# Routing tokens to experts in two parts, beside the experts' own work

## What is computed

```python
xm = layernorm(x) * gamma + beta                 # 6250 x 256
logits = xm @ Wr + br               # 8 experts, the best two of them per token
gate = softmax over the two chosen logits
y_k = gelu(xm @ W1[e_k] + b1[e_k]) @ W2[e_k] + b2[e_k]     # k = 1, 2; 256 -> 512 -> 256
out = x + gate_1 * y_1 + gate_2 * y_2
```

## Time and profile before

| what | value |
|---|---|
| median of 3 runs | 6035.27 us (6032.69 to 6035.34) |
| the profiled execution | 6032.18 us |
| its span, first to last instruction | 6030.5 us |
| granted TensorE clock, mean of the span | 0.766 of full speed |
| busy in the span | PE 55%, PEld 40%, DVE 46%, ACT 35%, POOL 62% |

### The profile page before, as it was taken

How to read it: one execution, slowest core, us unless ns; L and a number is a source line. 1 busy time by engine, 2 the same in 40 slices (tenths; PEclk the granted TensorE clock), 3 DMA queues, 4 the chain that set the end, 5 groups by cost and what they waited for, 6 DMA issues and landing times. The chain is left out here.

```text
span 6030.5 us, 75495 instructions
## 1 busy us (share of the span) xinstructions
PE 3346.5 (55%) x13479; PEld 2417.9 (40%) x13480; DVE 2750.8 (46%) x6682; ACT 2082.8 (35%) x5020; POOL 3748.8 (62%) x3707
## 2 busy tenths in 40 slices
PE   4355555555646666665834753056666664229990
PEld 1144444344434444443723752034444443216660
DVE  6655555532234444443544353555555557402223
ACT  4433333332333333332311310055555554313331
POOL 4266666666766666665777777777777773530006
PEclk7577777777967777777977987578888885569995
DMA  2233333333133333334211211011111115241114
GB/s 73 91 96 93 94 94 94 92 96 70 39 84 101 99 100 100 101 99 84 36 18 10 46 31 14 4 27 27 27 27 27 27 27 116 83 161 55 56 55 131
DMA packets 280618, 407.59 MB, mean 68 GB/s; under 512 B 93991, under 2 KB 197765, under 8 KB 280262
## 3 DMA queue, kind: packets, MB, share of 16 engines
q0 software_dynamic: 142720, 275.10, 19.7%
q1 hardware_dynamic: 137798, 131.50, 7.1%
HBM read 323.82 MB, written 81.61 MB: 67 GB/s over the span
## 5 line engine op out<-in xcount | busy, mean ns | idle before, releaser
L1156 PE MATMUL conv_ps<-conv_msg,conv_S 128*128 128x256 f32 x3328 | 1202.6, 536 | 991.6 <-DMA conv_msg<-relu_xn_table,GI 521.4
L1156 PEld LDWEIGHTS conv_ps<-conv_msg,conv_S 128*128 128x128 f32 x3328 | 907.0, 281 | 1314.5 <-issue 1121.2
L1128 DVE TENSOR_TENSOR ACC<-ACC,conv_ps 128x256 f32 x1664 | 700.9, 421 | 1190.0 <-PE conv_ps L1156 1082.6
L683 POOL DMA_INDIRECT edges_by_src<-packed,rank_i x800 | 953.9, 1192 | 308.9 <-issue 240.9
L1079 POOL DMA_INDIRECT conv_msg<-relu_xn_table,GI x832 | 800.4, 962 | 430.3 <-issue 235.3
L1079 POOL DMA_INDIRECT conv_msg<-conv_table,GI x832 | 788.2, 947 | 380.0 <-issue 233.9
L1852 POOL DMA_INDIRECT gat_msg<-attn_table,GI x832 | 824.9, 992 | 266.6 <-issue 253.3
L1099 ACT ACTIVATE conv_S<-iota_row,LOC 128x128 f32<-128x128 f32 x1664 | 507.9, 388 | 890.9 <-PE conv_ps L1156 806.2
L1905 PE MATMUL gat_ps<-gat_M,gat_S 128*128 128x260 f32 x1664 | 600.1, 509 | 373.9 <-DVE ACC L1959 223.4
L1905 PEld LDWEIGHTS gat_ps<-gat_M,gat_S 128*128 128x128 f32 x1664 | 378.6, 247 | 519.5 <-issue 463.1
L2508 POOL DMA_INDIRECT combine_y<-expert_out,combine_at x98 | 94.2, 961 | 578.5 <-ACTq L2496 557.2
(11 more groups left out here) (428 smaller groups left out, 5116.8 us busy)
## 6 DMA issues: line engine op xcount, KB each, us to landing
expert_in<-heads_zrow SPq DMA_DIRECT2D x53, 256.0 KB
experts_xe<-expert_in SPq DMA_DIRECT2D x106, 128.0 KB
expert_out<-experts_y SPq DMA_DIRECT2D x106, 128.0 KB, 1.7
conv_msg<-relu_xn_table,GI POOLq DMA_INDIRECT x832, 2.7
conv_msg<-conv_table,GI POOLq DMA_INDIRECT x832, 2.7
gat_msg<-attn_table,GI POOLq DMA_INDIRECT x832
edges_by_src<-packed,rank_i POOLq DMA_INDIRECT x800, 3.1
relu_xn_table<-begin_rx SPq DMA_DIRECT2D x49, 128.0 KB, 1.7
```

Source lines behind the costliest of these rows:

```text
L683: pool.indirect_dma_start(edges, bass.IndirectOffsetOnAxis(ap=m.rank_i[:, j:j + 1], axis=0), m.packed[:, j:j + 1], None).then_inc(sent[g % ...
L1128: nc.vector.tensor_tensor(acc, acc, ps[k % NB][:, 0:D], ALU.add).then_inc(added, 1)
L1156: nc.tensor.matmul(ps[k % NB][:, 0:D], S[:, h % 2, k, :], msg[:, h * RING + k, :], start=True, stop=True).then_inc(summed, 1)
```

## The change

The 49 row tiles are split into a first part of 25 and a second of 24 (`PART`). Each part has its own DRAM tables and its own padding: `EX_PART` is [58, 56], so there are 114 expert tiles instead of 106. The scan, the padding and the expert numbers are computed for each part in turn. The dispatch stage sends only the first part; its weights are issued from ScalarE's queue, beside it. In the experts stage, while the tiles of part one are worked, SyncE loads the second part's row tiles (one after every second expert tile) and GpSimd sends them. Once all 58 result tiles of part one are stored, GpSimd gathers the results of the first 24 row tiles (`BESIDE`), VectorE forms their sums between the tiles of part two (`collect`, after every second tile), and SyncE stores them. The combine stage does the remaining 25. The copies of positions into `at` are gone: the indirect DMAs read `pos_i` itself. SyncE's and GpSimd's lists are written out without loops.

```diff
-EX_TILES = ((2 * N + EXPERTS * (P - 1)) // P + 1) // 2 * 2
+PART = 25
+PART_ROWS = (PART * P, N - PART * P)
+EX_PART = [((2 * rows + EXPERTS * (P - 1)) // P + 1) // 2 * 2 for rows in PART_ROWS]
+EX_TILES = sum(EX_PART)
+BESIDE = 24
 RING = 8
...
-            rows = m.expert_in.rearrange("(t p a) d -> t p (a d)", p=P, a=2)
-            for k in range(EX_TILES // 2):
-                sp.dma_start(rows[k], zrow[:, :]).then_inc(zero_out, 16)
+            for h in range(2):
+                rows = m.expert_in[h].rearrange("(t p a) d -> t p (a d)", p=P, a=2)
+                for k in range(EX_PART[h] // 2):
+                    sp.dma_start(rows[k], zrow[:, :]).then_inc(zero_out, 16)
...
+            for h, (lo, hi) in enumerate(((0, PART), (PART, TILES))):
+                a, b, w, n = scan, other, 1, hi - lo
+                while w < n:
+                    v.drain()
...
+                nc.vector.tensor_scalar(cnt[:, :], a[:, hi - 1, :], float(P - 1), None, ALU.add)
+                nc.vector.tensor_tensor(pre[:, lo:hi, :], pre[:, lo:hi, :], a[:, lo:hi, :], ALU.add)
...
+                ex_lo, ex_n = sum(EX_PART[:h]), EX_PART[h]
+                nc.vector.tensor_tensor(sp8[:, :], x[:, :], nt[:, :], ALU.subtract)
+                nc.vector.tensor_tensor(cmp[:, 0:ex_n, :], x[0:1, :].unsqueeze(1).broadcast_to([1, ex_n, EXPERTS]),
+                                        m.iota_row[0:1, 0:ex_n].unsqueeze(2).broadcast_to([1, ex_n, EXPERTS]), ALU.is_le)
...
+                nc.vector.tensor_tensor(pre[:, lo:hi, :], pre[:, lo:hi, :],
+                                        sp8[:, :].unsqueeze(1).broadcast_to([P, n, EXPERTS]), ALU.add)
...
+def send_rows(nc, m, pool, i, xm, sent):
+
+    for k in range(2):
+        pool.indirect_dma_start(m.expert_in[part_of(i)], bass.IndirectOffsetOnAxis(ap=m.pos_i[0:rows_of(i), k, i:i + 1], axis=0),
+                                xm[0:rows_of(i), :], None).then_inc(sent, 16)
+
+
+def fetch_rows(nc, m, pool, i, pair, got):
+
+    for k, y in enumerate(pair):
+        pool.indirect_dma_start(y[0:rows_of(i), :], None, m.expert_out[part_of(i)],
+                                bass.IndirectOffsetOnAxis(ap=m.pos_i[0:rows_of(i), k, i:i + 1], axis=0)).then_inc(got, 16)
+
...
         def _(sp):
-            def load(i, s, rows):
-                if reused_of_four(i):
-                    sp.wait_ge(sent[s], 2 * dma_count_of_four(i - 4, s))
-                    held(sp, ts)
-                sp.dma_start(xm[s][:, :], m.xm[bass.ds(i * P, P), :]).then_inc(xm_in[s], 16)
-
-            over_tiles_by_four(sp, load)
+            for i in range(PART):
+                if i >= 4:
+                    sp.wait_ge(sent[i % 4], i // 4 * 32)
+                sp.dma_start(xm[i % 4][:, :], m.xm[i * P:(i + 1) * P, :]).then_inc(xm_in[i % 4], 16)
...
+        @block.scalar
+        def _(act):
             n = 0
             for e in range(EXPERTS):
                 for t, w, width in ((m.W1E, m.eW1, 2 * HID), (m.W2E, m.eW2, 4 * D)):
                     c = width // w.shape[2]
-                    sp.dma_start(t[:, e * width:(e + 1) * width].rearrange("p (c n) -> p c n", c=c),
-                                 w[e].rearrange("(c p) n -> p c n", p=P)).then_inc(w_in, 16)
+                    act.dma_start(t[:, e * width:(e + 1) * width].rearrange("p (c n) -> p c n", c=c),
+                                  w[e].rearrange("(c p) n -> p c n", p=P)).then_inc(w_in, 16)
                     n += 16
-            sp.dma_start(m.B1E[:, :], row_to_all(m.eb1.rearrange("e n -> (e n)"))).then_inc(w_in, 16)
...
+            for i in range(PART):
+                pool.wait_ge(xm_in[i % 4], 16 * (i // 4 + 1))
+                send_rows(nc, m, pool, i, xm[i % 4], sent[i % 4])
             for s in range(4):
-                pool.wait_ge(sent[s], 2 * 16 * ((TILES + 3 - s) // 4))
+                pool.wait_ge(sent[s], 32 * ((PART + 3 - s) // 4))
...
-            def tile(t, s):
-                if reused(t):
+                h, at = place_of(t)
+                sp.dma_start(m.expert_out[h][at, :], y[t % 2][:, :]).then_inc(stored[t % 2], 16)
+
+            def load_row_tile(k):
+                i = PART + k
+                if k >= 4:
+                    sp.wait_ge(sent[k % 4], k // 4 * 32)
+                sp.dma_start(xm[k % 4][:, :], m.xm[i * P:(i + 1) * P, :]).then_inc(xm_in[k % 4], 16)
+
+            def store_out(c):
+                sp.wait_ge(out_made, c + 1)
+                sp.dma_start(m.out[c * P:(c + 1) * P, :], o[c % 2][:, :]).then_inc(out_stored[c % 2], 16)
+
+            for t in range(EX_TILES):
+                if t >= 2:
                     sp.wait_ge(turned, t - 1)
-                    held(sp, ts)
-                sp.dma_start(xe[s][:, :], m.expert_in[bass.ds(t * P, P), :]).then_inc(x_in[s], 16)
-                if reused(t):
-                    store(t - 2, s)
-
-            in_twos(sp, EX_TILES, tile)
-            store(EX_TILES - 2, 0)
-            store(EX_TILES - 1, 1)
+                if t == EX_PART[0]:
+                    for k in range(4):
+                        sp.wait_ge(sent[k], 32 * ((TILES - PART + 3 - k) // 4))
+                h, at = place_of(t)
+                sp.dma_start(xe[t % 2][:, :], m.expert_in[h][at, :]).then_inc(x_in[t % 2], 16)
+                if t >= 2:
+                    store(t - 2)
+                if t % 2 == 1 and t // 2 < TILES - PART:
+                    load_row_tile(t // 2)
+                c = (t - EX_PART[0] - 5) // 2
+                if (t - EX_PART[0] - 5) % 2 == 0 and 0 <= c < BESIDE:
+                    store_out(c)
+            store(EX_TILES - 2)
+            store(EX_TILES - 1)
             for s in range(2):
                 sp.wait_ge(stored[s], EX_TILES * 8)
+                sp.wait_ge(out_stored[s], BESIDE * 8)
+
+        @block.gpsimd
+        def _(pool):
+            for k in range(TILES - PART):
+                pool.wait_ge(xm_in[k % 4], 16 * (k // 4 + 1))
+                send_rows(nc, m, pool, PART + k, xm[k % 4], sent[k % 4])
+            for s in range(2):
+                pool.wait_ge(stored[s], EX_PART[0] * 8)
+            for c in range(BESIDE):
+                if c >= 2:
+                    pool.wait_ge(out_made, c - 1)
+                fetch_rows(nc, m, pool, c, (y1[c % 2], y2[c % 2]), got[c % 2])
+            for s in range(4):
+                pool.wait_ge(sent[s], 32 * ((TILES - PART + 3 - s) // 4))
...
-            in_twos(v, EX_TILES, tile)
+            def collect(q, s):
+
+                v.wait_ge(got[s], q * 32 + 32)
+                if not (isinstance(q, int) and q == 0):
+                    v.wait_ge(out_stored[s], q * 16)
+                held(v, tv)
+                c = q * 2 + s
+                nc.vector.scalar_tensor_tensor(out=y1[s][:, :], in0=y1[s][:, :], scalar=m.gate[:, 0, bass.ds(c, 1)],
+                                               in1=m.X[:, bass.ds(c * D, D)], op0=ALU.mult, op1=ALU.add)
+                v.drain()
+                nc.vector.scalar_tensor_tensor(out=o[s][:, :], in0=y2[s][:, :], scalar=m.gate[:, 1, bass.ds(c, 1)],
+                                               in1=y1[s][:, :], op0=ALU.mult, op1=ALU.add).then_inc(out_made, 1)
+
+            def four(q):
+                for s in range(2):
+                    t = EX_PART[0] + s * 2 + q * 4
+                    tile(t, 0)
+                    tile(t + 1, 1)
+                    collect(q, s)
+
+            in_twos(v, EX_PART[0], tile)
+            four(0)
+            with v.Fori(1, BESIDE // 2) as q:
+                four(q)
+            with v.Fori((EX_PART[0] + BESIDE * 2) // 2, EX_TILES // 2) as q:
+                tile(q * 2, 0)
+                tile(q * 2 + 1, 1)
             out(EX_TILES - 1, 1, experts_of(DVE, EX_TILES - 1)[1])
...
+            for c in range(rest):
+                if c >= 4:
+                    pool.wait_ge(out_made, c - 3)
+                fetch_rows(nc, m, pool, BESIDE + c, (y1[c % 4], y2[c % 4]), got[c % 4])
```

More of the change, by code:

```diff
@@ L2529, in _ @@
         @block.sync
         def _(sp):
-            def tile(i, s, rows):
-                sp.wait_ge(out_made, i + 1)
-                held(sp, ts)
-                sp.dma_start(m.out[bass.ds(i * P, rows), :], o[s][0:rows, :]).then_inc(stored[s], 16)
-            over_tiles_by_four(sp, tile)
+            for c in range(rest):
+                i, s = BESIDE + c, c % 4
+                sp.wait_ge(out_made, c + 1)
+                sp.dma_start(m.out[i * P:i * P + rows_of(i), :], o[s][0:rows_of(i), :]).then_inc(stored[s], 16)
@@ L2537, in _ @@
             for s in range(4):
-                sp.wait_ge(stored[s], 16 * ((TILES + 3 - s) // 4))
+                sp.wait_ge(stored[s], 16 * ((rest + 3 - s) // 4))
 class Memory:
```

150 lines of the change are left out of this document (56 added, 94 removed).

## The result

The changed kernel takes **5941.4 us** (median of 3 runs, 5940.7 to 5942.5), against 6035.3 us before: a ratio of 0.985 with a 95% interval from 0.983 to 0.987, 94 us less. Forecast were 5945 us, in a range from 5926 to 5975. The profiled execution has a span of 5938.9 us where that of before has 6030.5, so 91.6 us are to be found in the two traces.

What follows compares the result with a forecast made beforehand. Four non-overlapping end stages, 842 of 6030.5 us: experts paced by TensorE, dispatch by GpSimd sends then weights, combine by GpSimd gathers, route by VectorE. Terms -72 + 38 + 1 - 61 + 4 + 0 = -90 us gave 5945 us, range 5926 to 5975.

Steps and rivals of the forecast that it cites:

- Combine: Last stage: 25 row tiles left of 49, 24 fewer at 2.52 us each, -61 us.
- Tiles: Experts stage: 114 tiles instead of 106, eight more at 4.76 us of TensorE-bound time, +38 us, called certain.
- What is laid beside the experts: Experts stage: added GpSimd issues, SyncE issues and VectorE collects stay hidden, cost 0, plus 1 us once at part two's start.
- the seam: Experts stage, between parts: GpSimd's first gather waits for tile 57's store, delaying the first collect, +1 us once.
- The steady cover of 0.6 us: Experts stage: VectorE time left before hb after a 1.1 us collect and register work, so collects cost 0.
- the prediction's own sum: Experts stage: xe load delayed by SyncE's extra issue, 0.2 + 2.06 + 0.4 said to just fit 2.61 us, cost 0.
- Route: Route tables: scan and padding run twice on half-size tiles on VectorE, +4 us, between 0 and +10.
- Heads: Ahead of the route: four more zero writes of 0.68 us on SyncE's queue, hidden, 0; uncovered, 3 us.
- Dispatch: Dispatch stage: 25 of 49 row tiles sent, weights beside them, 86 us, a gain of 72; ends 70 and 101 us.
- The ring: Dispatch: four row buffers turn in 18.2 us beside weights, 4.5 us a row tile instead of 2.56, for 42 us.
- rival of a clean overlap: Dispatch: weights delay no buffer and sends keep 1.28 us, stage 70 us, total 5929 us; chance 0.08.
- The slower rival: Experts, part two: waits drop TensorE to its lower clock, 4.4 us more a tile, total 6190 us; chance 0.03.

Runs made afterwards that it cites:

- run 6: Changed kernel with 12 instead of 24 row tiles collected beside the experts, on a slower chip: 6724.5 us, ratio 0.986 to the kernel before.
- run 5: Kernel before the change with 114 expert tiles instead of 106, on a slower chip: 6856.9 us, ratio 1.006 to the kernel before.
- run 7: Changed kernel with three more VectorE operations in each collect of part two, on a slower chip: 6721.8 us, ratio 0.984 to the kernel before.
- run 1: Changed kernel with the expert weights asked for only after the last send of the dispatch has landed: 5958.6 us.
- run 3: Changed kernel with eight row buffers in the dispatch instead of four: 5931.6 us.
- run 4: Changed kernel with dispatch and experts in one stage, no barrier between them: 5936.7 us.
- the second group: Four follow-up runs on a chip where every kernel takes about 13% longer; the kernel before the change took 6824.7 us there.

## Why the prediction was right

The total is 4 us from the measured one and each large term within 2 us, but one of them is right for partly wrong reasons.

*Combine* (-61): measured -61.4; run 6 gives 2.55 us a row tile where the earlier trace rows gave 2.52.

*Tiles* (+38): measured +38.9 alone in run 5, whose stage start is 0.3 us slower. The certain part was certain.

*What is laid beside the experts* (0 and +1 at the seam): measured 2.2 us. Against run 5 the start of the stage has 0.9 of it (the first y comes 17.6 us after the first xe load, in run 5 16.7, but 15.9 in the repeated profile of the changed kernel, so it is scatter), the first part 1.0 (272.7 us against 271.7, no more than the one wait for xe behind the short tile), and the second part with the seam and all collects 0.2 (265.9 against 265.7). GpSimd's gathers made VectorE wait once, at the seam. The steady cover of 0.6 us that I had left for the hb was 1.36 us: the register load that I set against it in full, here 0.64 us long, starts at 5620.5 under the collect's second operation and ends only some 0.3 us behind it. Run 7 shows that the cover was real and what would have come without it. For the xe load the prediction's own sum did not fit: 0.2 + 2.06 + 0.4 is 2.66 us, over the 2.61 it had to fit into. It held because the load comes no later than before (0.84 us after the store of y, where it was 0.95).

*Route* (+4): +4.1 on VectorE, 4.7 with the barriers. The half scan took 2.64 us where I had 2.4, the rest 4.65 where I had 4.6.

*Heads* (0): 57 zero writes, no change of the stage.

*Dispatch* (-72, to 86 us): measured -73.0, to 84.7 us. **Here three pieces of the sum were mis-sized and cancelled**, so that the closeness of this term is in part luck. (a) The ring. I had one turn as load 8.0 + two sends 2.56 + landing 7.6 = 18.2 us; the first turn took 13.9. The landing was 5.9 us, the load 13.9 - 5.9 - 1.3 = 6.7, and between the two sends there is only one issue distance, 1.3 us, since the landing is counted from the second one's issue. The rows for 7.6 us were four sends next to a burst of weight loads, too few: the nine sends from 5249 to 5266 have that median again, the sixteen ahead of them about 6. I also had the four buffers turn slowly for all of 42 us with 9 row tiles out; it was 25 sends, 12.5 row tiles, in 44 us. So the loss was 11.9 us and not 16. (b) The sends went out at 62.5 / 49 = 1.28 us as taken, but 50 sends have 49 steps (64 us were summed), and the first one came 2.8 us after its load was issued, not 3.6 after the stage's start. (c) The tail: the sum ended with the last landing. The trace of before does hold the 8.06 us of drain, under the weights, and I had costed the edit that takes this cover away at nothing. It costs 5.0 us, the first thing to be asked of a stage that now ends with software DMAs. Against the prediction's 86 us: -4.1 for the ring, -2.3 for the sends and the first of them, +5.0 for the tail; and in full 2.8 + 62.5 + 11.9 + 2.4 + 5.0 = 84.6. (The weights, taken at 31 us of all DMA engines, needed 32.5 in run 1. The share of 1.0 named in the prediction is 0.93 in its own rows.)

The Trainium skill, "DMA: Bandwidth & Descriptors", section "Issuing engines are not separate DMA queues", was the reason for the rival of a clean overlap, 70 us. The runs put it in its place. The engines are shared, as the page says: the share is 1.05 and a landing takes 5.9 us instead of 2.4. By the sum of loads alone the overlap should still have been clean, and with eight buffers it is (run 3: 72.4 us, of which 5.0 are drain and barrier, against the 70 worked out without these). So the sum of the loads did not decide here; the latency of each transfer, against four buffers, did.

*The slower rival*, TensorE at its lower clock in part two, did not happen: the granted clock is 1.00 from 5595 to 5861, and it stayed 1.00 in run 7 too, in which TensorE waited 21 us for hg.

## What to carry to other kernels

A bulk transfer laid beside a ring of small ones cost the ring latency here, not bandwidth: count the buffers against load + landing at full DMA load (6.7 + 1.3 + 5.9 us against 2.5 us a tile, which makes an estimate of six, not four; eight were run), or put the bulk where nothing else moves. When a change takes the last piece of work out of a stage, look in the trace for what ran hidden under it, drains and barriers included, and price it. And a stretch that is used to hide something has become a floor: shortening it afterwards gives nothing once it is shorter than what it hides.

## What the runs showed of the hardware that I had not expected

GpSimd's queue drains long after its last indirect DMA has landed: 4.13 us after 50 sends, the same to the nanosecond in seven profiles, and 8.06 us after 98, in the two kernels that have them. Behind the experts stage, in which 48 sends and 48 gathers ran, it took the first of these lines, and in run 4, where 98 sends and 48 gathers had been issued since the last stage's end, the second:

```profile
L50 POOLq DRAIN  x1: 10032/10032/10032, 5801.9 to 5801.9; - x1
```

```profile
L50 POOLq DRAIN  x1: 6591/6591/6591, 5797.7 to 5797.7; - x1
```

In run 6, with 48 sends and 24 gathers, it took 8.08 us. So it does not simply grow with the number of transfers, and what sets it stays open. In these kernels it was on the path only where nothing else was running at the end of the stage.

The chip of the second group took 754 us more for the same program ahead of the route stage. In the stages here the written-out loops of the changed kernel kept their length (dispatch from first send to first xe load 82.1 us against 81.9), while the dispatch and combine of the kernel before did not: in run 5 the same stretch of the dispatch took 171.7 us instead of 154.8, and the combine, from the last y, 158.7 instead of 139.4, with GpSimd's time of "issue" before its gathers at 33.5 us instead of 21.3. These two stages have register loops and ScalarE's copies into `at`, and the changed ones have neither; the experts stage of run 5, looped too, kept its length. Which of the two it is, was not tried.
